# A decoder layer on one core: group scores in one piece, another order of normalisation, queries stored by head, and a lead-in with three weight buffers

## The chip, the cores and the metric

The kernel runs on one core of one Trainium2 chip. The metric is the time of one execution in device microseconds (us). Profiles are of one execution each, with all times counted from the start of its span.

## The reference, cut to what matters

Eight sequences of 128 tokens with 512 features pass three residual blocks, each followed by a layer norm: a gated block with a polynomial part and a feed-forward part, cross-attention against a context, and a last feed-forward block. The change lies in the cross-attention:

```python
x = _rmsnorm(hidden_states, ln_weight)
h_q = (x @ w_q.T).reshape(b, lq, H, DH)                  # H = 32 heads of DH = 128
h_k = (key_value_states @ w_k.T).reshape(b, lk, H, DH)
h_v = (key_value_states @ w_v.T).reshape(b, lk, H, DH)
score = jnp.einsum('bqhd,bkhd->bhqk', h_q, h_k) + position_bias[None]
score = jnp.where(m, score, -jnp.inf)
score = jax.nn.softmax(score, axis=-1)
attn = jnp.einsum('bhqk,bkhd->bqhd', score, h_v).reshape(b, lq, H * DH)
return hidden_states + attn @ w_out.T
```

The inputs' mask leaves only keys among the last 32 of each sequence, and the kernel finds that out at run time. It then takes the branch `attention(few=True)`, the one that runs here.

## The kernel before

The eight sequences are two halves of four. The attention runs 64 head steps `n`: heads 0 to 15 of half 0 (n 0 to 15), the same heads for half 1 (n 16 to 31), heads 16 to 31 of half 1 (n 32 to 47), then of half 0 (n 48 to 63). In the first and third of these blocks (`shared(n)`), keys and values of both halves are computed at once; in the second and fourth (called late here) they come from what was kept, so those steps have no `keys` and `values` products, only semaphore steps. The last six steps of a late block ahead of a shared one have the keys of the heads to come.

Every engine walks an order written out by hand, a cycle per `n`. In cycle `n` TensorE (PE) has:

- `queries(n + 5)`: the small keys of a head times `wq`, in float32, into `bank[0]`. ScalarE (ACT) copies it to `t_ring` (`copy_queries`, L1133), with the head as the innermost index, so that consecutive elements are 16 bytes apart.
- `keys(n + 6)`: `few_hi`/`few_lo` times `wk_hi`/`wk_lo`, three products for each of four chunks, into `bank[1]`. It waits for the ACT copy of the bank (`copy_keys`), and for the two rounded parts of the weights: `split_k` on ACT (L1034) and `rest_k` on VectorE (DVE), made from `wk`, two buffers loaded by SyncE (SP).
- `turn(n - 1)` (L755) transposes the normalised probabilities, `weigh(n - 2)` (L822) adds to the output in `acc`, `outer(n - 1)` (L800) multiplies values and output weights, `values(n)` makes values.
- `group_scores`: the scores of four heads together (a group), 16 float32 products of 128 columns in `bank[2]` (32 passes, L728) on top of the bias (L706). With `j = n % 4`, the first half (part 0) stands at the end of the cycle `j == 2` and the second half (part 1) in the cycle `j == 3`, behind `queries`.

DVE, in cycle `n` with `m = n + 1`, has `add_mask(m)` (L1511; only for `m % 4 == 0` at this place, the others are done ahead), `find_max(m)` (L1517, L1519), then `divide(n)` (L1526 to L1532), then `rest_k` and more masks. `divide(n)` needs `exponentials(n)` of ACT (L1148), which follows `copy_outer(n - 2)` and `copy_values(n - 1)` in ACT's queue. `residual(2)` and `residual(3)` of DVE at n = 17 and n = 49 free `acc` for the next block.

The lead-in (n = -6 to -1) begins while the last tiles of the block before end: `chunk(0, 3)` of ACT, then `split_k(0)`, then on PE `keys(0)`, the last `down`, and cycles of `queries` and `keys`. SP's queue holds, ahead of it, ten loads of weights and biases, then the load of `ctxF` (the few keys of the context) into `a_raw[0]`; `split_few` (L1027) rounds it.

## Time and profile before

| what | value |
|---|---|
| median of 3 runs | 781.97 us (780.22 to 782.78) |
| the profiled execution | 781.2 us, span 779.4 us |
| PE busy | 724.6 us, 93% of the span |
| DVE busy | 528.5 us, 68% |
| ACT busy | 436.6 us, 56% |
| mean granted PE clock | 0.989 |

A busy PE is a modelled duration that contains the pipeline's latency, so an interval between starts tells more than the busy share. "Idle before" names what ended the idle time ahead of an instruction. In the chain that ended last, each row starts where the one before it released it; "issue" is time for which the profile shows no releaser.

### The profile page before, as it was taken

The page shows a single profiled execution, that of the slowest core. Times are in us where ns is not written, and L with a number is a line of the kernel's source. Part 1 is how long each engine was busy: PE and PEld are TensorE (multiplying, and loading weights), DVE is VectorE, ACT ScalarE, POOL GpSimd, SP SyncE. Part 2 cuts the span into 40 slices and gives each one's busy share as a digit, 9 for nine tenths or more (in the row PEclk, how much of TensorE's full clock was granted, in tenths as well). Part 3 has the DMA queues.
Part 4 walks back from the last instruction along what each step waited for, and adds up shares of the span by engine and source line. Part 5 has one row for each costly group of instructions (what it writes and reads, how often), then busy time and mean ns, then how long its engine had stood idle before and what let it go on. Part 6 is the DMA issues. An engine that isn't in the chain of part 4 may idle for free.

```text
span 779.4 us, 12293 instructions
## 1 busy us (share of the span) xinstructions
PE 724.6 (93%) x4082; PEld 558.9 (72%) x4082; DVE 528.5 (68%) x912; ACT 436.6 (56%) x747; POOL 95.6 (12%) x84
## 2 busy tenths in 40 slices
PE   8999999999978999999989999999989779998994
PEld 6788888888868777765556777876545347886883
DVE  6556687577645786468776668656986737578655
ACT  6333233333346787777776777667767454554452
POOL 2000000190007300000000000000040002304503
PEclk9999999999999999999999999999999999999998
DMA  8555441466735665678886676566875512442631
GB/s 317 161 226 181 137 147 56 150 202 200 242 122 181 200 215 177 202 232 273 263 282 198 214 244 196 188 219 227 279 252 181 158 68 81 154 136 87 212 133 54
DMA packets 70681, 145.10 MB, mean 186 GB/s; under 512 B 7920, under 2 KB 8192, under 8 KB 69984
## 3 DMA queue, kind: packets, MB, share of 16 engines
q1 hardware_dynamic: 69200, 137.26, 54.0%
q0 software_dynamic: 1200, 6.70, 2.2%
q8 instruction: 34, 0.56, 0.3%
q10 hardware_dynamic: 224, 0.39, 0.2%
q14 instruction: 23, 0.19, 0.1%
HBM read 142.23 MB, written 2.10 MB: 185 GB/s over the span
## 4 chain that ended last, share of the span: by engine, by line
PE 74%; DVE 14%; issue 4%; DMA 3%; ACT 2%; SPq 1%; POOL 1%; ACTq 0%; DVEq 0%; POOLq 0%
PE bank L524 34%; PE acc L524 14%; PE bank L728 7%; PE acc L822 6%; PE bank L693 5%; PE bank L800 5%; DVE score L1511 2%; DVE score L1519 2%; DVE neg_max L1517 2%; DVE row_sum L1526 2%; DVE prob L1532 1%; PE bank L706 1%; DMA a_raw<-ctxF 1%; DVE a_lo L1260 1%; DMA b_raw<-b 1%
## 5 line engine op out<-in xcount | busy, mean ns | idle before, releaser
L524 PE MATMUL bank<-feat_hi,a_hi 128*128 128x512 f32 x348 | 137.4, 395 | 3.2 <-DVE a_lo L1260 1.2
L524 PE MATMUL bank<-feat_lo,a_hi 128*128 128x512 f32 x348 | 136.3, 392 | 2.4 <-issue 2.4
L1260 DVE TENSOR_TENSOR a_lo<-a_raw,a_hi 128x1024 fp32r<-128x1024 f32 (+3 forms) x47 | 56.8, 1208 | 99.1 <-ACT a_hi L974 88.0
L1511 DVE TENSOR_TENSOR score<-bank,mask_add 128x512 f32<-128x512 f32 x64 | 42.5, 685 | 79.6 <-PE bank L728 79.6
L524 PE MATMUL acc<-b_hi,tile_hi 128*128 128x512 f32 x224 | 87.8, 392 | 4.1 <-DVE tile_lo L1260 2.2
L1133 ACT ACTIVATE t_ring<-bank 128x512 f32<-128x512 f32 x64 | 70.4, 1101 | 32.7 <-PE bank L693 32.7
L524 PE MATMUL acc<-b_hi,tile_lo 128*128 128x512 f32 x224 | 87.2, 389 | 0.0
L524 PEld LDWEIGHTS bank<-feat_hi,a_hi 128*128 128x128 f32 x348 | 65.8, 189 | 23.8 <-issue 4.3
L822 PE MATMUL acc<-u_sb,prob_t 32*128 32x512 f32 x512 | 77.2, 646 | 0.4 <-DVE resid L1368 0.4
L524 PEld LDWEIGHTS bank<-feat_lo,a_hi 128*128 128x128 f32 x348 | 65.8, 189 | 13.5
L991 ACT ACTIVATE tile_hi<-pair 128x512 fp32r<-128x512 f32 x54 | 33.9, 628 | 67.0 <-DVE pair L1322 37.3
L524 PE MATMUL bank<-feat_hi,a_lo 128*128 128x512 f32 x180 | 70.1, 390 | 0.0
L432 POOL TENSOR_SCALAR scale<-moments 128x4 f32<-128x4 f32 (+1 forms) x9 | 2.1, 233 | 542.2 <-DVEq L1390 542.0
L728 PE MATMUL bank<-t_ring,xn 128*128 128x128 f32 x512 | 62.2, 275 | 0.0
L728 PEld LDWEIGHTS bank<-t_ring,xn 128*128 128x128 f32 x512 | 60.9, 192 | 1.3
L1167 ACT ACTIVATE u_sb<-bank 128x512 f32<-128x512 f32 x64 | 38.3, 598 | 32.3 <-PE bank L800 29.6
L524 PE MATMUL acc<-b_lo,tile_hi 128*128 128x512 f32 x136 | 52.9, 389 | 0.0
L524 PEld LDWEIGHTS acc<-b_hi,tile_hi 128*128 128x128 f32 x224 | 42.2, 188 | 14.4 <-DVE b_lo L1260 3.3
L1000 ACT ACTIVATE gated<-bank 128x512 f32<-128x512 f32 x20 | 11.9, 598 | 67.8 <-PE bank L524 67.8
L1260 DVE TENSOR_TENSOR b_lo<-b_raw,b_hi 128x512 fp32r<-128x512 f32 x56 | 40.0, 715 | 14.1 <-ACT b_hi L981 13.8
L981 ACT ACTIVATE b_hi<-b_raw 128x512 fp32r<-128x512 f32 x56 | 34.8, 624 | 26.0 <-PE acc L524 21.3
L1141 ACT ACTIVATE prob_t<-bank 128x512 f32<-128x512 f32 x64 | 40.4, 631 | 15.5 <-PE bank L755 15.5
(149 smaller groups left out, 1580.2 us busy)
## 6 DMA issues: line engine op xcount, KB each, us to landing
wk<-ax SPq DMA_DIRECT2D x64, 256.0 KB, 3.5
wqi<-ax SPq DMA_DIRECT2D x64, 256.0 KB, 3.3
wq<-wqn SPq DMA_DIRECT2D x64, 256.0 KB, 3.7
wv<-wvh SPq DMA_DIRECT2D x64, 256.0 KB, 3.6
wo<-bx SPq DMA_DIRECT2D x64, 256.0 KB, 3.6
a_raw<-w SPq DMA_DIRECT2D x22, 512.0 KB, 4.1
a_raw<-a SPq DMA_DIRECT2D x21, 512.0 KB, 5.3
b_raw<-b SPq DMA_DIRECT2D x34, 256.0 KB, 2.6
```

The lines of the kernel that those rows point to most:

```text
L524: mm = pe.matmul(out_ap, w, x, start=start and k == 0, stop=stop and k == len(products) - 1, skip_group_check=True)
L693: mm = pe.matmul(bank[0][:, c * P:(c + 1) * P], wq[par][:, c * P:(c + 1) * P], few_keys, start=True, stop=True)
L728: mm = pe.matmul(bank[2][:, b * P:(b + 1) * P], xn[half][:, c, b * SEQ:(b + 1) * SEQ], t_ring[g % 2][:, c, b, :, :].rearrange("p k h -> p ...
L800: mm = pe.matmul(bank[1][:], few_values, wo[slot][:], start=True, stop=True)
L822: mm = pe.matmul(acc[b][:], prob_t[par][rows, 0:P], u_sb[par][rows, :], start=begins, stop=ends, skip_group_check=True)
L981: act.activation(b_hi[par][:], b_raw[par][:], ACT.Copy).then_inc(b_hi_ok, 1)
L991: act.activation(tile_hi[par][:], src, ACT.Copy).then_inc(tile_hi_ok, 1)
L1133: act.activation(t_ring[n // GH % 2][:].rearrange("p c b k h -> p (c b k h)")[:, n % GH:GH * N:GH], bank[0][:], ACT.Copy).then_inc(t_ok, 1)
L1141: act.activation(prob_t[n % 2][:], bank[3][:], ACT.Copy).then_inc(turned_ok, 1)
L1167: act.activation(u_sb[n % 2][:], bank[1][:], ACT.Copy).then_inc(u_ok, 1)
L1260: return dve.tensor_tensor(out_ap, whole, high, ALU.subtract)
L1511: dve.tensor_tensor(score[n % GH][:], bank[2][:].rearrange("p (b k) -> p b k", b=HB), mask_add[j][:, half * HB:(half + 1) * HB, :], ALU.ad ...
```

## The change

Nothing is computed differently; the order, the layout and the buffers change.

1. `group_scores` is one piece at the end of the cycle `j == 2`, ahead of the `queries` of the next cycle.
2. DVE has `divide(n)` ahead of `add_mask(n + 1)` and `find_max(n + 1)` where `n + 1` begins a group.
3. `t_ring` is stored head by head, so ACT writes 512 neighbouring elements; the scores' product reads it so, and writes its 128 columns into `bank[2]` with a step of four elements (16 bytes).
4. Lead-in: `wk` gets a third buffer (`gated`, free by then), so `load_k(n)` runs three ahead; the keys of n = 1, 3, 5 go to `bank[3]`; `keys` stands ahead of `queries` and waits for the copy of two steps before; `split_k`/`rest_k` run two steps ahead; on SP, `ctxF` stands behind four loads and not behind ten.

```diff
-WO_RING = 4
+WO_RING, WK_RING = 4, 3
+def keys_in(n):
+    return 3 if n < LEAD_K and n % 2 == 1 else 1
-        t_ring = two("t_ring", [P, C, HB, FEW, GH])
+        t_ring = two("t_ring", [P, GH, C, HB, FEW])
+        wk.append(gated)
 def load_k(n):
-                if n >= 2:
-                    sp.wait_ge(k_mm, n - 1)
-                sp.dma_start(wk[n % 2][:], ax[head_of(n)][:, D:]).then_inc(wk_dma[n % 2], 16)
+                if n == WK_RING - 1:
+                    sp.wait_ge(hidden_ok, HALVES * F1)
+                if n >= WK_RING:
+                    sp.wait_ge(k_mm, n - WK_RING + 1)
+                sp.dma_start(wk[n % WK_RING][:], ax[head_of(n)][:, D:]).then_inc(wk_dma[n % WK_RING], 16)
 # SP, ahead of the loop
-            for n in range(2):
-                load_k(n)
-                load_q(n)
-                load_v(n)
-                load_o(n)
-                load_bias(n)
+            load_k(0)
+            load_q(0)
+            load_k(1)
             sp.wait_ge(a_lo_ok, A30)
             sp.dma_start(a_raw[0][:], ctxF).then_inc(few_dma, 16)
-            for n in range(2, WO_RING):
+            load_q(1)
+            for n in range(2):
+                load_v(n)
+                load_bias(n)
+            load_o(0)
+            load_k(2)
+            for n in range(1, WO_RING):
                 load_o(n)
 # SP, in the loop
-                if 2 <= n + LEAD_K + 2 < HN:
-                    load_k(n + LEAD_K + 2)
+                if WK_RING <= n + LEAD_K + WK_RING < HN:
+                    load_k(n + LEAD_K + WK_RING)
 # PE, keys(n)
                     if n == 0:
                         pe.wait_ge(hidden_ok, HALVES * F1)
+                    elif n == 1:
+                        pe.wait_ge(xn_ok, C)
                     else:
-                        pe.wait_ge(k_ok, n)
-                        pe.wait_ge(kept_k_ok, shared_count(n - 1))
+                        copied = n if n >= LEAD_K else n - 1
+                        pe.wait_ge(k_ok, copied)
+                        pe.wait_ge(kept_k_ok, shared_count(copied - 1))
 # PE, group_scores
-                    for b in range(2 * part, 2 * part + 2):
+                    for b in range(HB):
                         for c in range(C):
-                            mm = pe.matmul(bank[2][:, b * P:(b + 1) * P], xn[half][:, c, b * SEQ:(b + 1) * SEQ],
-                                           t_ring[g % 2][:, c, b, :, :].rearrange("p k h -> p (k h)"), start=False, stop=(c == C - 1),
+                            mm = pe.matmul(bank[2][:, b * P:(b + 1) * P].rearrange("p (k h) -> p h k", h=GH),
+                                           xn[half][:, c, b * SEQ:(b + 1) * SEQ], t_ring[g % 2][:, :, c, b, :], start=False, stop=(c == C - 1),
                                            skip_group_check=True)
 # PE, the order of a cycle
+                    if n < 0:
+                        keys(n + LEAD_K)
                     if 0 <= n + LEAD_T < HN:
                         queries(n + LEAD_T)
-                    if few and j == 3 and n >= -1 and g + 1 < HALVES * GROUPS:
-                        group_scores(g + 1, 1)
-                    if not late and n + LEAD_K < HN:
+                    if n >= 0 and not late and n + LEAD_K < HN:
                         keys(n + LEAD_K)
                     if few and j == 2 and g + 1 < HALVES * GROUPS and n >= -2:
-                        group_scores(g + 1, 0)
+                        group_scores(g + 1)
 # ACT
-                act.activation(t_ring[n // GH % 2][:].rearrange("p c b k h -> p (c b k h)")[:, n % GH:GH * N:GH], bank[0][:],
-                               ACT.Copy).then_inc(t_ok, 1)
+                act.activation(t_ring[n // GH % 2][:, n % GH].rearrange("p c b k -> p (c b k)"), bank[0][:], ACT.Copy).then_inc(t_ok, 1)
             split_k(0)
+            split_k(1)
             few_bias_heads()
-                if late and n + LEAD_K < HN and not shared(n + LEAD_K):
+                if n < 0 or late and n + LEAD_K < HN and not shared(n + LEAD_K):
                     copy_keys(n + LEAD_K)
+                if n < 0:
+                    split_k(n + LEAD_K + 2)
                 if 0 <= n + LEAD_T < HN:
                     copy_queries(n + LEAD_T)
-                if n + LEAD_K + 1 < HN and shared(n + LEAD_K + 1):
+                if n > 0 and n + LEAD_K + 1 < HN and shared(n + LEAD_K + 1):
                     split_k(n + LEAD_K + 1)
 # DVE
-                if 0 <= m < HN:
-                    if m % GH == 0:
-                        add_mask(m)
+                if 0 <= m < HN and m % GH > 0:
                     find_max(m)
                 if n >= 0:
                     divide(n)
-                if n + LEAD_K + 1 < HN and shared(n + LEAD_K + 1):
+                if 0 <= m < HN and m % GH == 0:
+                    add_mask(m)
+                    find_max(m)
+                if n < 0:
+                    rest_k(n + LEAD_K + 2)
+                elif n > 0 and n + LEAD_K + 1 < HN and shared(n + LEAD_K + 1):
                     rest_k(n + LEAD_K + 1)
```

## Rows read from the trace of the kernel before

**Rows 1.** The page: busy time, share of the span and instructions of each engine
```profile
PE 724.6 (93%) x4082; PEld 558.9 (72%) x4082; DVE 528.5 (68%) x912; ACT 436.6 (56%) x747; POOL 95.6 (12%) x84
```
**Rows 2.** Busy us (count) by stretch: PE, PEld, DVE, ACT, POOL; clock, DMA share, GB/s
```profile
262.00:347.50 85.50, 83.51 (x608) 65.76 (x605) 57.88 (x109) 63.41 (x122) 0.56 (x2) 1.00 0.65 207
347.50:434.40 86.90, 80.29 (x514) 54.27 (x514) 63.54 (x122) 61.29 (x108) 0.00 (x0) 1.00 0.77 252
...
541.40:630.60 89.20, 76.54 (x455) 45.45 (x453) 68.17 (x133) 57.84 (x99) 9.59 (x6) 0.98 0.62 202
```
**Rows 3.** Chain that ended last, one late group: start us, us, what
```profile
373.48 0.70 DVE score L1511
...
385.44 0.39 PE bank L755
...
388.43 1.78 PE bank L728 x16
390.22 0.89 PE bank L693 x8
...
392.93 0.70 DVE score L1511
```
**Rows 4.** Timeline of DVE in that group: start, us, line, op
```profile
375.54 0.68 DVE L1526 TENSOR_REDUCE row_sum<-prob 128x4 f32<-128x512 f32 x1
...
377.27 0.68 DVE L1511 TENSOR_TENSOR score<-bank,mask_add 128x512 f32<-128x512 f32 x1
```
**Rows 5.** Timeline of ACT: exponentials of the first head of groups 4 and 5
```profile
356.15 0.62 ACT L1148 ACTIVATE prob<-score 128x512 f32<-128x512 f32 x1
...
376.69 0.63 ACT L1148 ACTIVATE prob<-score 128x512 f32<-128x512 f32 x1
```
**Rows 6.** The chain, where group 4's scores are read
```profile
351.99 0.70 DVE score L1511
```
**Rows 7.** Pieces of the chain without a releaser, ahead of `values` and of `keys`
```profile
333.56 0.58 issue
...
419.03 1.59 issue
```
**Rows 8.** Timeline of PE, first cycle of the second shared block
```profile
444.24 0.39 PE L755 MATMUL bank<-ident_r,prob 128*128 128x128 f32 x1 [0.83 <-DVE prob L1532]
```
**Rows 9.** Group 13: DVE's timeline at its scores, then the chain five cycles on
```profile
567.39 0.69 DVE L1511 TENSOR_TENSOR score<-bank,mask_add 128x512 f32<-128x512 f32 x1 [1.35 <-PE bank L728]
...
581.24 1.87 PE acc L822 x8
```
**Rows 10.** Timelines of the lead-in: ACT, PE, then DVE at the first scores
```profile
217.81 1.06 ACT L1027 ACTIVATE a_hi<-a_raw 128x1024 fp32r<-128x1024 f32 x1 [3.43 <-DMA a_raw<-ctxF]
...
221.30 0.67 ACT L1017 ACTIVATE xn<-bank,const 128x512 f32<-128x512 f32 x1
...
223.46 0.55 PE L524 MATMUL bank<-a_hi,wk_hi 128*128 128x256 f32 x1 [3.50 <-DVE wk_lo L1260]
...
247.49 0.69 DVE L1511 TENSOR_TENSOR score<-bank,mask_add 128x512 f32<-128x512 f32 x1 [4.14 <-PE bank L728]
```
**Rows 11.** The chain in the lead-in: queries, a load, queries two cycles on
```profile
232.36 1.16 PE bank L693 x8
...
234.98 3.54 DMA wk<-ax
...
239.88 1.16 PE bank L693 x8
```
**Rows 12.** Groups by line, op and tile: busy us, mean ns, idle before
```profile
L1133 ACT ACTIVATE t_ring<-bank 128x512 f32<-128x512 f32 x64 | 70.4, 1101 | 32.7 <-PE bank L693 32.7
L728 PE MATMUL bank<-t_ring,xn 128*128 128x128 f32 x512 | 62.2, 275 | 0.0
L1126 ACT ACTIVATE k_ring<-bank 128x512 f32<-128x512 f32 x64 | 38.1, 595 | 0.0
L524 PE MATMUL bank<-a_hi,wk_lo 128*128 128x256 f32 x128 | 36.6, 286 | 0.0
```

More of the change, by code:

```diff
@@ L210, in decoder_kernel @@
         wqi_dma, wq_dma = [sem("wqi_dma0"), sem("wqi_dma1")], [sem("wq_dma0"), sem("wq_dma1")]
-        wk_dma, wv_dma = [sem("wk_dma0"), sem("wk_dma1")], [sem("wv_dma0"), sem("wv_dma1")]
+        wk_dma, wv_dma = [sem(f"wk_dma{i}") for i in range(WK_RING)], [sem("wv_dma0"), sem("wv_dma1")]
         wo_dma = [sem(f"wo_dma{i}") for i in range(WO_RING)]
@@ L646, in keys @@
                 def keys(n):
-                    half, par = half_of(n), n % 2
-                    pe.wait_ge(wk_dma[par], 16 * (n // 2 + 1))
+                    half, par, raw = half_of(n), n % 2, n % WK_RING
+                    keys_bank = bank[keys_in(n)]
+                    pe.wait_ge(wk_dma[raw], 16 * (n // WK_RING + 1))
                     if shared(n):
@@ L665, in keys @@
                         if few:
-                            mm = passes(bank[1][:, 0:HALVES * P], wk_hi[par][:, chunk], wk_lo[par][:, chunk],
+                            mm = passes(keys_bank[:, 0:HALVES * P], wk_hi[par][:, chunk], wk_lo[par][:, chunk],
                                         few_hi[:, c, :], few_lo[:, c, :], c == 0, c == C - 1)
                         else:
-                            mm = pe.matmul(bank[1][:], wk[par][:, chunk], ctx_raw[half][:, c * N:(c + 1) * N],
+                            mm = pe.matmul(keys_bank[:], wk[raw][:, chunk], ctx_raw[half][:, c * N:(c + 1) * N],
                                            start=(c == 0), stop=(c == C - 1))
@@ L743, in head_scores @@
                     for b in range(HB):
-                        mm = pe.matmul(bank[2][:, b * P:(b + 1) * P], t_ring[g % 2][:, b, :, :, j].rearrange("p b k -> p (b k)"),
+                        mm = pe.matmul(bank[2][:, b * P:(b + 1) * P], t_ring[g % 2][:, j, b, :, :].rearrange("p b k -> p (b k)"),
                                        k_ring[:, n % RING, b * SEQ:(b + 1) * SEQ], start=False, stop=True, skip_group_check=True)
@@ L765, in values @@
                     if n == 0:
-                        pe.wait_ge(xn_ok, C)
+                        pe.wait_ge(k_ok, LEAD_K)
+                        pe.wait_ge(kept_k_ok, LEAD_K)
                     else:
@@ L1029, in split_k @@
             def split_k(n):
-                act.wait_ge(wk_dma[n % 2], 16 * (n // 2 + 1))
+                act.wait_ge(wk_dma[n % WK_RING], 16 * (n // WK_RING + 1))
                 if n >= 2:
                     act.wait_ge(k_mm, n - 1)
-                act.activation(wk_hi[n % 2], wk[n % 2][:], ACT.Copy).then_inc(wk_hi_ok, 1)
+                act.activation(wk_hi[n % 2], wk[n % WK_RING][:], ACT.Copy).then_inc(wk_hi_ok, 1)
             def split_v(n):
@@ L1122, in copy_keys @@
                         act.wait_ge(t_mm, n - BLOCK + 1)
-                    act.activation(kept_k[n % BLOCK], bank[1][:, other * P:(other + 1) * P], ACT.Copy).then_inc(kept_k_ok, 1)
+                    act.activation(kept_k[n % BLOCK], bank[keys_in(n)][:, other * P:(other + 1) * P], ACT.Copy).then_inc(kept_k_ok, 1)
                 if n >= RING:
                     act.wait_ge(score_mm, n - RING + 1)
-                act.activation(k_ring[:, n % RING, :], bank[1][:], ACT.Copy).then_inc(k_ok, 1)
+                act.activation(k_ring[:, n % RING, :], bank[keys_in(n)][:], ACT.Copy).then_inc(k_ok, 1)
             def copy_queries(n):
@@ L1186, in _ @@
                     chunk(2, 2 * (n - FEATURES_2), bank[0])
-                if not late and n + LEAD_K < HN:
+                if n >= 0 and not late and n + LEAD_K < HN:
                     copy_keys(n + LEAD_K)
@@ L1501, in _ @@
             rest_k(0)
+            dve.wait_ge(tile_lo_ok, T30)
+            rest_k(1)
             few_bias_rests()
```

20 lines of the change are left out of this document (9 added, 11 removed).

## The prediction

> **What bounds the kernel now.** I first read the busy time of the page: PE 93%, DVE 68%, ACT 56% [rows 1]. That is a mean over stages, so the stretches come next [rows 2]. In the first shared block PE is busy for 83.5 of 85.5 us. In the late blocks it is busy for 80.3 of 86.9 us and 76.5 of 89.2 us, while DVE has 63.5 and 68.2 us of work: neither is full, so they wait for each other in turn. The chain shows how [rows 3]: a group's scores end, DVE reads them at 373.48, stays on the chain until 385.44 when PE can transpose, PE then runs up to the next scores, which DVE reads at 392.93. One turn of this loop is 392.93 - 373.48 = 19.45 us. It contains two things that the change takes out of it: DVE's `divide` of the last head of the old group, and PE's `queries` between the two halves of the scores. The lead-in has its own loop of loads, rounding and copies [rows 10, 11].
>
> **The late loop.** `divide` goes ahead of `add_mask`. It costs 377.27 - 375.54 = 1.73 us of DVE [rows 4], and fits into the time in which DVE waits for the scores now. What it needs, the exponentials of that head, come from ACT while PE has the scores to do. So 1.73 us leave the chain. `queries` (390.22 to 391.11, 0.89 us) stand ahead of the second half now [rows 3]; behind the scores they are in nobody's way at first: another 0.89 us, 2.62 together.
>
> Part of it is given back. The `queries` now delay the `turn`, `weigh` and `outer` behind them by 0.89 us against the end of the scores. ACT's exponentials of the new group's first head stand behind the copy of that `outer`. They begin at 376.69 and take 0.63, so they end 3.8 us after the scores are read [rows 3, 5]. With 0.89 more that is 4.7 to 4.8 us. DVE wants them after `add_mask`, `find_max`, one more `add_mask` and one more `find_max`; in today's order the `divide` of 1.73 us lies between and it asks at 379.32 - 373.48 = 5.84 us, in the new order at 4.1. It waits 0.65 us. Net 2.62 - 0.65 = 1.97 us per boundary.
>
> Not all boundaries are like that one. By groups:
>
> - Scores of groups 6, 7 and 15 as the next ones (three regular loops): 3 x 1.97 = 5.9.
> - Groups 5 and 13: the cycle behind the scores belongs to a shared head, with `values` ahead of `outer`. There the exponentials end at 356.15 + 0.62, 4.8 us after the read at 351.99 [rows 5, 6]; 0.89 more makes 5.7 against a demand at 4.1, so 1.57 us come back: 2 x 1.05 = 2.1.
> - Group 8 (the last of a late block): `keys` waits 1.59 us for rounded weights that DVE makes behind `divide` [rows 7]. Those are ready in time once the DVE loop is shorter. I take 1.6, and PE is the bound from there on.
> - First shared cycle after it: `turn` sat 0.83 us for DVE's probabilities [rows 8], 1.0 with its latency. That goes.
> - Group 14: `residual(3)` and `variances(2)` fill DVE ahead of the scores. It is idle for only 1.35 us before them [rows 9], less than the 1.73 + 0.89 it would need. Net 1.35. The same loop has a `weigh` of 1.87 us where 1.07 is usual, with the granted clock at 0.98 [rows 2, 9]. PE ran at its lower level there, after a row of waits. I count half of that cost of 1.6 us as regained: 0.8.
> - After the last scores no `queries` are left and no wait comes back: 1.7.
>
> Sum of the late loop: 5.9 + 2.1 + 1.6 + 1.0 + 1.35 + 0.8 + 1.7 = 14.5 us. PE does not cut it: the stretch 347.5 to 434.4 loses 6.6 us by this, as much as it shows PE idle, and a PE counted as busy holds latency besides.
>
> **Queries by head.** A copy of one bank to neighbouring places takes 595 ns; `t_ring` takes 1101 [rows 12]. So each of the 64 copies gains 0.5 us, all on ACT. ACT has room (61 of 87 us [rows 2]), so most of them are worth nothing. The exception is a head step with `values` and no `keys`, where `values` waits 0.58 us for the copy of `turn`, which ACT does behind `t_ring` [rows 7]. The chain has three such pieces before the first late block and four before the second: 7 x 0.5 = 3.5. One more copy lies on the chain near n = 10: 0.5. Together 4.0 us.
>
> The other side of this layout is the product itself, which now writes with a step of 16 bytes in PSUM. No row shows such a write. What rows show is the pace: 16 passes of 128 float32 columns take 1.79 us [rows 3], 112 ns each and 0.87 ns a column, while the float32r product of `keys` runs 256 columns within a duration of 286 ns against 275 for these 128 [rows 12]: float32 columns come at about half the float32r pace. The nearest row for a step of 16 bytes is ACT's, 1101 against 595, a factor of 1.85. If that factor sits on the write's own pace, it disappears under the slower float32 columns and costs nothing. If it multiplies the pass, it costs 512 x 112 ns x 0.85 = 49 us. I take nothing and keep the other as a rival. The read of `t_ring` stays in runs of 32 neighbours.
>
> The Trainium skill speaks against this edit ("PSUM — Partial Sum Buffer", section "Specifications (TRN2)"): cachelines of 8 bytes, and "any non-contiguous AP slows matmuls significantly". By it the sum would come out slower than before, as in the rival of that name; no row here shows such a write.
>
> **The lead-in.** PE is idle 3.50 us up to 223.46, waiting for `rest_k(0)`, behind ACT's copy at 221.30, behind the `split_few` that waited 3.43 us for `ctxF` [rows 10]. With six loads fewer ahead (SP issues one in about 0.45 us) it lands in time, and what is late next is PE's last transposes, just before PE fell idle at 219.96. The copy behind them starts 1.3 us sooner, `keys(0)` 1.5 sooner with its `split_k` right behind.
>
> After that, two cycles take 239.88 - 232.36 = 7.52 us now, 3.76 each, in a loop with one load of 3.54 us [rows 11]. With the third buffer a load is asked for a cycle sooner, but on SP it stands behind `load_q`, which waits for `queries`. Issues 0.85, load 3.54, two roundings 1.3, semaphores 0.1: 5.8 us for two cycles, 2.9 each. The cycle of the last `down` is PE's own in both. Three cycles gain 0.85 each, 2.5 us. The first late load (n = 4) holds ACT's queue, with `copy_queries` behind it, for about 1.7 us. Net 1.5 + 2.5 - 1.7 = 2.3 us. From nothing (the lower clock lasts as long as now, or the wait on `hidden_ok` at the head of SP's queue holds `wo` loads) to 4.0.
>
> Moving `load_k(2)` behind a wait on `hidden_ok` queues three `wo` loads and the loop behind it; their first reader is `outer(1)`, which comes after the first scores (247.49 [rows 10]), so it costs nothing. The other reordered loads are read no sooner than in the second cycle.
>
> **Sum.** 14.5 + 4.0 + 2.3 = 20.8 us, against the profiled execution of 781.2 us: 760.4. The median of three runs lies 0.8 above it: about 761 us. The bounds of the gains alone are 11 us (no lead-in gain, no regained clock, exponentials half a microsecond later at each boundary) and 30 us (full 2.62 at all nine boundaries, 4 in the lead-in): 752 to 771.
>
> **Rivals.**
> 1. *The stepped write slows the scores.* One place, 512 passes, all on the path in shared blocks where PE is full. At ACT's factor: 781.97 + 49 - 20.8 = 810 us; it decides from 20.8/512 = 41 ns a pass, 112 becoming 153. For it: no contiguous run is left in a write. Against it: half pace of float32. Chance 0.14.
> 2. *Half of the gain.* DVE's loop shortens, but another wait takes its place: the exponentials behind `outer` in ACT's queue, since each boundary has only 1.97 left of 2.62 by my count. If all ACT copies there slip by another microsecond, nine boundaries lose 9 us: 770 to 776. Chance 0.13. No change within 0.3%, which is about what a measurement can tell here: 0.03.
> 3. *More than the sum.* With fewer waits PE keeps its higher clock everywhere and the lead-in gains 4 us: 750 to 754. Chance 0.10.
> 4. *The forecast*, 754 to 769: chance 0.60.
>
> Faster 0.83, same 0.03, slower 0.14. The likeliest case spans 754 to 769; I give 751 to 771.
>
> **What the profile of the changed kernel would show.** `t_ring` copies near 0.60 us on ACT. Scores as 32 passes in about 3.57 us, mean 275 ns; if the mean is nearer 400 or the 32 passes take over 5 us, rival 1 holds. DVE's wait for the scores near 2 us with `row_sum` ahead of it, and a short wait for ACT's exponentials in its place. The late loop at 17.5 us for 19.45. The 0.58 us pieces gone. The first `keys` at about 222 us, the first `add_mask` 2 to 3 us before 247.5. The prediction is wrong if the passes slow, or if the late loop stays above 18.5 us.

## The result, and the profile after

The changed kernel takes 770.77 us (median of 4 runs, 767.9 to 770.99) against 782.38 us for the kernel before on the same chip (780.22 to 783.97): a ratio of 0.9845, 95% interval 0.9811 to 0.9879. It is faster by 11.6 us where 20.8 were forecast. The profiled execution took 770.99 us, with a span of 769.2 us and a mean granted clock of 0.983. Against the profiled execution of before that is 10.2 us of span.

The first lines of the page after, engines with busy time and share, answer to [rows 1]:

```profile
PE 724.1 (94%) x4082; PEld 561.6 (73%) x4082; DVE 534.2 (69%) x912; ACT 407.1 (53%) x747; POOL 93.4 (12%) x84
```

ACT has 30 us less to do, which is the copy of `t_ring` and little else. The windows of the same three stages as in [rows 2], placed by the new starts (columns as there):

```profile
264.00:348.00 84.00, 83.38 (x609) 65.31 (x609) 60.35 (x111) 57.52 (x122) 0.57 (x2) 1.00 0.64 207
349.00:430.10 81.10, 78.35 (x514) 53.93 (x514) 64.41 (x122) 53.91 (x108) 0.00 (x0) 1.00 0.80 273
535.00:618.50 83.50, 73.63 (x454) 44.74 (x453) 68.55 (x133) 52.30 (x99) 9.77 (x6) 1.00 0.64 215
```

PE was idle for 6.6 us of the first late block before and is for 2.8 us now, and the last stretch has the full clock where it had 0.98. So the middle of the kernel did about what was forecast in kind. Where the time went is plainest from a table by stage, worked out from the timelines: each entry is when the stage's first instruction starts, in us from the start of the span. "Scores 4" is the bias product ahead of the scores of group 4.

| start of | before | after | gained since the line above |
|---|---|---|---|
| last transposes ahead of the attention | 209.79 | 210.86 | -1.07 |
| first `keys` | 223.46 | 223.47 | +1.06 |
| first `turn` | 255.49 | 258.54 | -3.04 |
| scores 4 | 346.47 | 347.96 | +1.56 |
| scores 5 | 367.95 | 368.50 | +0.94 |
| scores 6 | 387.51 | 386.98 | +1.08 |
| scores 7 | 408.99 | 406.41 | +2.05 |
| scores 8 | 433.36 | 429.11 | +1.67 |
| scores 12 | 540.38 | 533.98 | +2.15 |
| scores 13 | 561.86 | 554.51 | +0.95 |
| scores 14 | 584.12 | 574.84 | +1.93 |
| scores 15 | 603.87 | 593.13 | +1.46 |
| first tile of the last block | 630.58 | 618.50 | +1.34 |
| end of the span | 779.4 | 769.2 | -1.88 |

Three stages do not fit the sum. The lead-in, from the first `keys` to the first `turn`, loses 3.0 us. A regular late loop (scores 5 to scores 6) gains 1.08 and not 1.97. The end gives 1.9 us back. The first two are followed up below.

What the stepped write and the new `t_ring` cost stands in the lines of the page after (operation, busy us, mean ns, idle before):

```profile
L741 PE MATMUL bank<-t_ring,xn 128*128 128x128 f32 x512 | 61.4, 279 | 0.0
L1147 ACT ACTIVATE t_ring<-bank 128x512 f32<-128x512 f32 x64 | 38.1, 596 | 42.8 <-PE bank L707 42.8
L1543 DVE TENSOR_REDUCE row_sum<-prob 128x4 f32<-128x512 f32 x64 | 43.7, 683 | 30.6 <-ACT prob L1161 29.1
L1528 DVE TENSOR_TENSOR score<-bank,mask_add 128x512 f32<-128x512 f32 x64 | 42.5, 684 | 17.6 <-PE bank L741 17.6
```

The copy fell from 1101 to 596 ns [rows 12]. The mean of the scores' passes is 279 ns where it was 275 before. Those 4 ns come from one group of scores in the lead-in that ran at a low clock (below). In the other groups the 32 passes take 3.57 us, as the two pieces of 16 in 1.78 us did before [rows 3]: the write with a step of 16 bytes costs nothing here. DVE used to wait 79.6 us for scores, as this line of the page of before says:

```profile
L1511 DVE TENSOR_TENSOR score<-bank,mask_add 128x512 f32<-128x512 f32 x64 | 42.5, 685 | 79.6 <-PE bank L728 79.6
```

Now it waits 17.6 us for them, and 29.1 us for ACT's exponentials ahead of `row_sum`. That is the change of waits that the prediction named, and in the late loop it has the size that was forecast:

```profile
377.90 0.69 DVE L1543 TENSOR_REDUCE row_sum<-prob 128x4 f32<-128x512 f32 x1 [0.58 <-ACT prob L1161]
```

DVE reads group 5's scores at 373.13 us, and these exponentials end at 377.86 us, 4.73 us later (4.7 to 4.8 forecast). DVE waits 0.58 us for them (0.65 forecast).

**The late loop after.** The chain that ended last, from one group's scores to the next (start, us, what), answers to [rows 3]:

```profile
369.52 3.57 PE bank L741 x32
373.09 0.89 PE bank L707 x8
...
375.17 1.07 PE bank L813 x2
376.24 0.02 issue
376.26 0.02 ACT u_sb L1180
...
376.75 0.60 ACT v_sb L1173
377.36 0.09 issue
377.45 0.36 PE bank L767
...
387.81 3.57 PE bank L741 x32
```

There is no DVE on it any more. ACT is on it three times a group, between `outer` (L813) and the next `turn` (L767). PE's own timeline shows what that costs:

```profile
377.45 0.36 PE L767 MATMUL bank<-ident_r,prob 128*128 128x128 f32 x1 [0.33 <-ACT v_sb L1173]
381.15 0.36 PE L767 MATMUL bank<-ident_r,prob 128*128 128x128 f32 x1 [0.33 <-ACT v_sb L1173]
```

From one `turn` to the next is 381.15 - 377.45 = 3.70 us. In the 1.21 us between the end of `outer` (376.24) and `turn`, PE has its `queries` to do, and then stands idle for 0.33 us. Meanwhile ACT copies `outer`'s product to `u_sb` and behind it, in its queue, bank 3 to `v_sb`, and `turn` waits for that second copy. In a late cycle nobody reads `v_sb`: `outer` takes `kept_v`. The program issues the copy all the same, and `turn`, which writes into the same bank, waits for its semaphore. I had not priced this queue position. I had priced the exponentials one place further back in it.

**The lead-in after.** PE's timeline, with the idle time before and its releaser in brackets:

```profile
223.47 0.36 PE L534 MATMUL bank<-a_hi,wk_hi 128*128 128x256 f32 x1 [2.44 <-DVE wk_lo L1275]
237.14 1.13 PE L707 MATMUL bank<-k_ring,wq 128*128 128x128 f32 x8 [1.59 <-ACT t_ring L1147]
...
243.76 0.50 PE L720 MATMUL bank<-a_hi,ident_r 128*128 128x512 f32 x1 [2.52 <-ACT t_ring L1147]
```

The first idle time is 2.44 us in place of 3.50 [rows 10]. But PE now waits for the copies of `t_ring`, and the chain says why these are late:

```profile
230.89 0.91 PE bank L707 x8
231.82 0.33 SPq L296
...
232.66 3.19 DMA wk<-ax
235.88 0.03 ACT wk_hi L1047
236.41 0.59 ACT t_ring L1147
237.14 1.14 PE bank L707 x8
239.15 3.42 DMA wk<-ax
242.59 0.63 ACT wk_hi L1047
243.22 0.49 ACT t_ring L1147
...
244.49 5.20 PE bank L741 x32
```

`queries` (L707) release `load_q` on SP (L296), behind which `load_k` is issued, whose 3.2 to 3.4 us of DMA hold `split_k` on ACT (L1047), behind which stands the copy of `queries`, for which PE waits. At 242.59 ACT rounds weights that no `keys` need for two steps, while the first scores wait for a copy that was ready to run. Then the scores take 5.20 us for the 32 passes that take 3.57 elsewhere. The granted clock tells why:

```profile
240.00:252.00 12.00, 9.37 (x62) 8.95 (x62) 3.48 (x6) 2.58 (x7) 11.22 (x10) 0.86 0.36 117
```

Its PEclk is 0.86, a mean over the two levels of 2.4 and 1.2 GHz; from 244 to 250 us, around the passes alone, it is 0.72. PE had been idle for 2.52 us just before the scores.

### The profile page after: what moved, and what is told of

The parts are those of the page before. It is cut to its first block, busy times and chain, and to the rows that moved or that the text cites. A ratio compares the mean times of both kernels' runs of the same rounds, so it can differ in the third digit from the quotient of the medians.

```text
span 769.2 us, 12295 instructions
## 1 busy us (share of the span) xinstructions
PE 724.1 (94%) x4082; PEld 561.6 (73%) x4082; DVE 534.2 (69%) x912; ACT 407.1 (53%) x747; POOL 93.4 (12%) x84
## 4 chain that ended last, share of the span: by engine, by line
PE 85%; DVE 5%; issue 3%; DMA 3%; ACT 3%; POOL 1%; SPq 1%; ACTq 0%; DVEq 0%; POOLq 0%
PE bank L534 37%; PE acc L534 16%; PE acc L835 8%; PE bank L741 8%; PE bank L813 7%; PE bank L707 5%; PE bank L767 1%; ACT v_sb L1173 1%; PE bank L720 1%; DMA b_raw<-b 1%; PE bank L566 1%; DMA wk<-ax 1%; DMA a_raw<-a 1%; POOL resid L509 1%; DVE b_lo L1275 0%
## 5 line engine op out<-in xcount | busy, mean ns | idle before, releaser
L534 PE MATMUL acc<-b_hi,tile_hi 128*128 128x512 f32 x224 | 89.5, 399 | 3.9 <-DVE tile_lo L1275 2.0
L835 PE MATMUL acc<-u_sb,prob_t 32*128 32x512 f32 x512 | 74.9, 640 | 0.0
L1543 DVE TENSOR_REDUCE row_sum<-prob 128x4 f32<-128x512 f32 x64 | 43.7, 683 | 30.6 <-ACT prob L1161 29.1
L1147 ACT ACTIVATE t_ring<-bank 128x512 f32<-128x512 f32 x64 | 38.1, 596 | 42.8 <-PE bank L707 42.8
L1528 DVE TENSOR_TENSOR score<-bank,mask_add 128x512 f32<-128x512 f32 x64 | 42.5, 684 | 17.6 <-PE bank L741 17.6
L1180 ACT ACTIVATE u_sb<-bank 128x512 f32<-128x512 f32 x64 | 38.2, 598 | 29.1 <-PE bank L813 26.4
L534 PEld LDWEIGHTS acc<-b_hi,tile_lo 128*128 128x128 f32 x224 | 42.9, 192 | 8.9
```

Of the source, the lines that this page charges most:

```text
L534: mm = pe.matmul(out_ap, w, x, start=start and k == 0, stop=stop and k == len(products) - 1, skip_group_check=True)
L835: mm = pe.matmul(acc[b][:], prob_t[par][rows, 0:P], u_sb[par][rows, :], start=begins, stop=ends, skip_group_check=True)
L1147: act.activation(t_ring[n // GH % 2][:, n % GH].rearrange("p c b k -> p (c b k)"), bank[0][:], ACT.Copy).then_inc(t_ok, 1)
L1180: act.activation(u_sb[n % 2][:], bank[1][:], ACT.Copy).then_inc(u_ok, 1)
L1528: dve.tensor_tensor(score[n % GH][:], bank[2][:].rearrange("p (b k) -> p b k", b=HB), mask_add[j][:, half * HB:(half + 1) * HB, :], ALU.ad ...
L1543: dve.tensor_reduce(row_sum[:], prob[n % 2][:], AX_X, ALU.add).then_inc(sum_ok, 1)
```

## The experiments: each part alone

Four kernels share one chip and one median of before (782.07 us). Each undoes or does one part. The first keeps the parts 1 to 3 and has the lead-in of before.

```diff
 # oldlead: the kernel before, with the scores in one piece, divide first, t_ring by head; WK_RING = 2, the old order of loads, keys and queries
 # divide: the kernel before, with this alone, on DVE
-                if 0 <= m < HN:
-                    if m % GH == 0:
-                        add_mask(m)
-                    find_max(m)
+                if 0 <= m < HN and m % GH > 0:
+                    find_max(m)
                 if n >= 0:
                     divide(n)
+                if 0 <= m < HN and m % GH == 0:
+                    add_mask(m)
+                    find_max(m)
 # together: the kernel before, with group_scores in one piece at the end of the cycle j == 2, and nothing else
 # layout: the kernel before, with t_ring [P, GH, C, HB, FEW], ACT's copy in 512 neighbours, and the scores' product written with the step of four
```

> Parts 1 to 3 with the lead-in of the kernel before. Theory L (the new lead-in costs time: ACT holds copy_queries behind split_k, which waits for wk, and PE falls to its lower clock): about 2 us faster than the changed kernel, near 769 us, first turn near 255 us. The ledger on record (the new lead-in gains 2.3): 2.3 us slower than the changed kernel, near 773.

> Only the divide of the old group ahead of add_mask. The ledger: 1.73 us less at each late boundary and no wait for the exponentials (3.8 against a demand at 4.1 us): 9 x 1.5 us, near 769. Theory V (in late cycles turn waits for the copy of v_sb, which stands behind the copy of u_sb in ACT's queue, so the loop PE, ACT is nearly as long as DVE's): less than half of it, 4 to 6 us, near 777.

> Only the scores of a group in one piece. The ledger: 0.89 us at each boundary where DVE's chain binds, exponentials still in time: 8 us, near 774. Theory V: the same, since the DVE chain still has the divide in it; a gain under 3 us speaks for another bound.

> Only t_ring by head and the stepped write of the scores. The ledger: 4 us (seven waits of 0.58 us shortened, one copy), near 778. Rival that the stepped write slows the scores: over 5 us a group for 32 passes, slower than 790; the changed kernel's trace already shows 3.57, so this should repeat. Also possible: the faster ACT queue helps late cycles too (v_sb sooner), then 775 or less.

| kernel | median us | ratio to before (95%) | first `turn` at | first `turn` to last block |
|---|---|---|---|---|
| before | 782.07 | | 255.49 | 375.09 |
| oldlead | 766.62 | 0.9798 (0.9766 to 0.9831) | 254.95 | 361.57 |
| divide | 769.35 | 0.9847 (0.9823 to 0.9871) | 253.44 | 363.52 |
| together | 775.66 | 0.9926 (0.9898 to 0.9955) | 256.08 | 369.37 |
| layout | 779.39 | 0.9965 (0.9944 to 0.9986) | 256.58 | 370.15 |

The expectations, each with its result:

- oldlead: the theory that the new lead-in costs time gave 769 us with the first `turn` near 255 us, the sum on record gave 773. It took 766.62 us, with the first `turn` at 254.95. The first theory holds, and the sum's +2.3 falls.
- divide: 769 by the sum, 777 if `turn` and `v_sb` already bound nearly as much. It took 769.35 us. With DVE still carrying the loop, the wait for `v_sb` is not yet the limit.
- together: 774 forecast, 775.66 measured.
- layout: 778 forecast, 779.39 measured.

Two things follow. First, the kernel without the new lead-in is 4 us faster than the one with it: 766.62 against 770.77. The scores of group 1 begin at 264.62 against 268.37 us, those of group 5 at 364.75 against 368.50: 3.75 us apart at both places, so the difference was made ahead of them. Second, between the first `turn` and the last block the parts gain 11.6, 5.7 and 4.9 us alone, 22.2 together, and 13.5 us when they are all there. Part of that difference is the clock and not the parts. Between the scores of group 13 and those of 14 the granted clock was 0.94 in before and 0.93 in oldlead, and 1.00 in divide, together, layout and the changed kernel. So that one loop counts 1.94, 1.31 and 1.32 us in the three kernels with one part and only 0.46 us in oldlead. Without it the parts gain 9.6, 4.4 and 3.6 us alone, 17.7 together, against 13.1 us in oldlead and 13.2 us in the changed kernel. The overlap is thus 4.5 us. The loop from scores 5 to scores 6 shows it: 19.56 us before, 18.92 in divide, 18.92 in together, 19.43 in layout and 18.50 in oldlead. Each part shortens the same loop, and another limit is reached when the first of them is in.

The layout alone gives 4.9 us there, and that this is close to the 4.0 of the prediction is in part luck: 3.25 us come where they were forecast (first `turn` to scores 4, and scores 8 to 12), 1.3 us from the clock between scores 13 and 14. Its passes of 128 columns are written with the step and its total is not slower. A part of divide's time over the whole is luck: its lead-in has the code of before, and its first `turn` came 2 us earlier, with a granted clock of 1.00 from 222 to 228 us where before had 0.72. The stretch behind the first `turn` leaves that out.

## The experiments: the lead-in

Two kernels take the changed kernel and move one step in one queue each.

```diff
 # copyfirst: ACT, in the loop; the copy of queries no longer waits behind the rounding that waits for a load
-                if n < 0:
-                    split_k(n + LEAD_K + 2)
                 if 0 <= n + LEAD_T < HN:
                     copy_queries(n + LEAD_T)
+                if n < 0:
+                    split_k(n + LEAD_K + 2)
 # loadfirst: SP, in the loop; load_k no longer waits behind load_q, which waits for queries
+                if n < 0:
+                    load_k(n + LEAD_K + WK_RING)
                 if 2 <= n + LEAD_T + 2 < HN:
                     load_q(n + LEAD_T + 2)
-                if WK_RING <= n + LEAD_K + WK_RING < HN:
+                if 0 <= n and n + LEAD_K + WK_RING < HN:
                     load_k(n + LEAD_K + WK_RING)
```

> The changed kernel, in the lead-in with copy_queries ahead of split_k in ACT's queue. Theory Q (PE's 5.6 us of waits for the t_ring copy come from that copy standing behind a split_k that waits for its load): the four waits go, the first scores start 2 to 3 us sooner, PE may keep its clock there; 768 to 766 against 770.8. Theory D (the loop of loads binds, the order of ACT only moves the wait to keys and wk_lo): within 1 us of the changed kernel.

> The changed kernel, in the lead-in with load_k ahead of load_q in SP's queue. Theory D: the loads of wk start as soon as keys are done and not after queries plus two issues, 1.5 to 2.5 us sooner per load, so split_k waits for none: 3 to 4 us faster than the changed kernel, near 767. Theory Q: also faster, since split_k then waits for nothing and the copy behind it goes through; the two theories differ in the run with the other order, not in this one. If the lower clock alone is the cause, within 1 us.

The kernel with the copy first took 766.79 us (ratio 0.9791, 0.9756 to 0.9825), the one with the load first 763.18 us (0.9753, 0.9730 to 0.9777; before 782.89). The first scores began at 241.41 and 240.40, against 243.76. With the load first the same place of the chain reads:

```profile
241.13 3.57 PE bank L743 x32
```

and the window of that stretch:

```profile
240.00:252.00 12.00, 10.55 (x87) 10.30 (x88) 6.97 (x12) 6.14 (x12) 11.55 (x10) 1.00 0.53 170
```

The 32 passes take 3.57 us again and the granted clock is 1.00. In copyfirst the window from 240 to 252 us has 1.00 too. With the copy first, theory Q came true (scores 2.4 us sooner, 766 to 768 us), and theory D's "within 1 us" fell: a copy behind a rounding that waits for a load is what held PE. With the load first the gain was larger than either theory's 767 us. Its first `turn` came 5.6 us sooner than in the changed kernel, and some 2.8 us of the profile came in the last block, for a reason that has nothing to do with the lead-in (see the end of the span, below). Both moves mend the same wait, and either does most of it.

The third buffer was worth about what the prediction gave it, once the load is not queued behind another: the first `turn` stands at 252.99 us against 254.95 with the old lead-in, 2.0 us. The medians differ by more, 763.18 and 766.62 us, but were taken on two chips, and oldlead's profile holds the low clock between scores 13 and 14.

## The experiments: the late loop

My next idea was that the late loop is held by `outer` and its copy, ahead of `values`, and that the order of the shared cycles (`values` first, then `outer`) would free it. This was run on the kernel with the old lead-in (values_first), and on the changed one with both moves of the lead-in (all_three).

```diff
 # values_first (and all_three): PE
-                    if late:
-                        outer(n - 1)
                     if 0 <= n < HN:
                         values(n)
-                    if n >= 1 and not late:
+                    if n >= 1:
                         outer(n - 1)
 # ACT
-                if late:
-                    copy_outer(n - 1)
                 if n >= 0:
                     copy_values(n)
-                if n >= 1 and not late:
+                if n >= 1:
                     copy_outer(n - 1)
```

> Parts 1 to 3 with the old lead-in, and in late cycles values ahead of outer on PE and copy_values ahead of copy_outer on ACT. Theory V (turn waits for the v_sb copy behind the u_sb copy): a late loop of 18.5 us becomes 16.8 to 17.5, some 6 to 9 us over the eight late loops: 758 to 761 against 766.6. The ledger (exponentials and DVE bind, V is no bound): within 1 us of 766.6, since the exponentials stay behind the copy of outer.

> The changed kernel with all three orders: copy_queries first, load_k first, values first. If the new lead-in's loss is the two queue orders and its third buffer is worth anything, it ends below values_first by 1 to 3 us. If the third buffer is worth nothing, it equals values_first.

Both fell short. The first took 775.30 us (0.9912, 0.9879 to 0.9945; before 782.89), 8.7 us more than oldlead, and the second 773.61 us (0.9881, 0.9856 to 0.9907), 1.7 us below values_first as expected, but slower than the changed kernel in spite of the mended lead-in. A regular loop became 19.72 us in values_first, where it is 18.48 with the order of the changed kernel. Its chain:

```profile
375.64 0.51 issue
376.15 1.10 PE bank L798 x2
...
378.28 0.36 PE bank L753
```

`outer` (L798) starts 0.51 us after `weigh` each time, and the chain shows no releaser. In the code `values(n)` now stands ahead of it, which in a late cycle is only semaphore steps, one of them a wait for the copy of `turn` to `prob_t`. ACT's timeline has that copy behind those of `k_ring` and `t_ring`, ending at 375.80 us:

```profile
375.19 0.61 ACT L1134 ACTIVATE prob_t<-bank 128x512 f32<-128x512 f32 x1
375.88 0.60 ACT L1153 ACTIVATE v_sb<-bank 128x512 f32<-128x512 f32 x1
```

`outer` follows at 376.15 us. From one `turn` to the next this makes 378.28 - 374.22 = 4.06 us out of 3.70: in the old place `outer` was the work that covered this copy. So PE's old order was not what held the loop, and the new one lengthens it.

This loop is not the whole loss. Of the 10.9 us between oldlead and values_first from the first `turn` to the last block, 6.1 us lie behind the last scores, where PE's granted clock was low:

```profile
612.00:626.30 14.30, 10.25 (x33) 4.61 (x29) 6.23 (x13) 5.57 (x11) 0.00 (x0) 0.52 0.25 92
```

In those last cycles the edit also moves `outer` behind the `features` products, and its copy behind `chunk`. Whether that or something else lowered the clock there is not shown.

What was left of the theory was ACT's own order. Two kernels test that alone: v_early, on top of both_orders (both moves of the lead-in), and narrow_v, on top of loadfirst.

```diff
 # both_orders: the changed kernel with copyfirst and loadfirst
 # v_early: both_orders, and on ACT
-                if late:
-                    copy_outer(n - 1)
                 if n >= 0:
                     copy_values(n)
+                if late:
+                    copy_outer(n - 1)
 # narrow_v: loadfirst, and in copy_values on ACT
-                act.activation(v_sb[n % 2][:], bank[3][:], ACT.Copy).then_inc(v_ok, 1)
+                width = N if shared(n) else 1
+                act.activation(v_sb[n % 2][:, 0:width], bank[3][:, 0:width], ACT.Copy).then_inc(v_ok, 1)
```

> The changed kernel with load_k first and copy_queries first. Theory D and Q together: all_three had its first turn 1 us sooner than loadfirst; 1 us less than loadfirst, near 762. If the orders overlap fully, 763.

> loadfirst with the v_sb copy of late cycles cut to one column (this leaves out a copy whose values nothing reads in this branch). Theory V (in late cycles turn waits for the v_sb copy behind the u_sb copy): the regular late loop of 18.5 us falls to the 17.5 of the ledger, where exponentials and DVE bind; some 6 us less in all, near 757 against 763.2. If the loop stays at 18.5, the wait put down to v_sb is another one.

> The changed kernel with load_k first, copy_queries first, and only on ACT the late copy_values ahead of copy_outer (PE keeps its order; its semaphore step for values is issued while outer still runs). Theory V: the v_sb copy runs under outer, turn finds it done, the late loop falls to 17.5; with 1 us from the lead-in, 755 to 757. Against it: v_sb's copy waits for PE's step and for the turned copy and delays the u_sb copy, as in values_first; then 18.5 or more and over 762.

| kernel | median us | ratio to before (95%) | regular late loop us | first `turn` to last block us |
|---|---|---|---|---|
| both_orders | 764.37 | 0.9776 (0.9760 to 0.9793) | 18.49 | 359.97 |
| narrow_v | 761.08 | 0.9743 (0.9720 to 0.9766) | 17.88 | 356.70 |
| v_early | 760.44 | 0.9727 (0.9710 to 0.9745) | 17.73 | 356.36 |

The moved copy gives 3.6 us behind the first `turn`, most of it in the two late blocks, and the copy cut to one column 3.1 us against loadfirst (359.84). The bank and the semaphore are the same in all of them, so the cost is the time at which this copy ends: its place behind another and its length. The mechanism holds; its size was put too high. Six us and a loop of 17.5 us were expected, and 755 to 757 us in all. The loops in front of scores 5 and 8 gained nothing by the move (20.53 and 22.69 us).

v_early against all_three tests PE's order: ACT has `copy_values` ahead of `copy_outer` in both, and only all_three has `values` ahead of `outer` on PE (with `copy_outer` behind `chunk` in the last cycles). They take 760.44 and 773.61 us. Both moves of the lead-in together are no better than the load first alone (764.37 against 763.18, where 762 to 763 were expected), which agrees with their mending one wait. The chain of v_early over a loop:

```profile
363.12 3.57 PE bank L743 x32
...
369.83 0.89 PE bank L709 x8
370.72 0.14 issue
370.86 0.36 PE bank L769
...
380.85 3.57 PE bank L743 x32
```

From these scores to the next takes 17.73 us, and PE is on the chain throughout but for some 0.3 us. ACT's copy to `v_sb` now comes first:

```profile
372.52 0.60 ACT L1175 ACTIVATE v_sb<-bank 128x512 f32<-128x512 f32 x1
373.38 0.60 ACT L1182 ACTIVATE u_sb<-bank 128x512 f32<-128x512 f32 x1 [0.27 <-PE bank L815]
```

This is the fastest kernel of the study: 760.44 us, 10.3 us below the changed one, with three places in a queue moved. In a regular late loop little is left but PE's own products, so with this work on PE it is close to the floor.

## The experiment: the stepped write

The scores' passes are float32, and the argument that a slow write would disappear under them says nothing about faster products. So the kernel with the load first was given stepped writes at two more places: `outer`'s product of 512 float32 columns with a step of 16 bytes, and the float32r product of `keys` in runs of two elements 32 bytes apart. The columns land in another order at both places, so this kernel does not compute the reference's output and serves for its times alone.

```diff
-mm = pe.matmul(bank[1][:], few_values, wo[slot][:], start=True, stop=True)
+mm = pe.matmul(bank[1][:].rearrange("p (k h) -> p h k", h=GH), few_values, wo[slot][:], start=True, stop=True)
-mm = passes(keys_bank[:, 0:HALVES * P], wk_hi[par][:, chunk], wk_lo[par][:, chunk],
+mm = passes(keys_bank[:, 0:HALVES * P].rearrange("p (k h d) -> p h k d", h=4, d=2), wk_hi[par][:, chunk], wk_lo[par][:, chunk],
```

> loadfirst with two more products that write with a step: outer (float32, 512 columns) with the scores' step of 16 bytes, and keys (float32r, 256 columns) in runs of two elements, 32 bytes apart; the columns land in another order, so the output is not the reference's. Theory H (float32 columns are so slow that a stepped write hides): outer's two passes stay at 0.86 us, and keys, at the full pace, may slow. If the stepped write costs by itself, outer's passes grow too, by up to the factor 1.85. If runs of two are free at full pace, keys stays at 1.43 us for 12 passes.

One execution: 763.9 us, with a span of 762.1 (loadfirst 760.7). The lines of the stepped kernel:

```profile
L815 PE MATMUL bank<-wo,v_sb 128*128 128x512 f32 x64 | 32.8, 594 | 0.0
L536 PE MATMUL bank<-a_hi,wk_lo 128*128 128x256 f32 x128 | 36.1, 282 | 0.0
```

and the same of the kernel with contiguous writes:

```profile
L815 PE MATMUL bank<-wo,v_sb 128*128 128x512 f32 x64 | 32.8, 594 | 0.0
L536 PE MATMUL bank<-a_hi,wk_lo 128*128 128x256 f32 x128 | 36.3, 284 | 0.0
```

594 and 594 ns, 282 and 284 ns. Since the ends of products are modelled, the intervals are the better witness, and they agree: in the chains of both kernels `outer`'s two passes take 0.86 us in the shared blocks, the products of `keys` start 0.12 us apart, and from the scores of group 1 to those of group 15 it is 324.76 us stepped and 324.77 us contiguous. Neither product notices. The 1.4 us between the spans is not from the products: the first `turn` comes 1.4 us sooner in the stepped kernel, and its last block is 2.8 us longer.

So a step of 16 bytes slowed neither of the float32 products here. Whether the slow pace of float32 hides it, as the prediction argued, is not shown: the float32r form, at twice that pace, did not slow either, but each of its runs fills eight bytes. A float32r write of single elements with a step was not tried.

## Why the prediction was right or wrong

**Direction and range: right.** 770.77 us lies within 751 to 771, 0.2 us from its upper edge. The gain is 11.6 us of 20.8. That it ended on this side of the edge is luck: two things that no part of the change sets, the clock between scores 13 and 14 and the idle stretch in the last block, move the time by 1.5 us and by up to 3 us. The time is that of its second rival (770 to 776), and so is the reason in kind: the loop shortens, and another wait takes its place in ACT's queue. That rival named the exponentials. They came as late as the sum had them and no later, and what came was the copy to `v_sb`.

**Which part holds, by its own steps.**

- *A boundary as 2.62 minus 0.65, 1.97 us net.* The step that failed in the late loop: it counted what stands in ACT's queue in front of the exponentials, and not in front of `turn`. Once DVE is off the chain, `turn` waits for `v_sb` behind `u_sb`, three times a group. Measured 1.08 us for group 6, 2.05 for 7 and 1.46 for 15, in sum 4.6 for 5.9; only group 7 gave what was forecast, and its loop is no regular one (it has the `keys` of the heads to come, 21.48 us before). The forecast loop of 17.5 us was 18.48 us from scores to scores, and 18.28 by DVE's reads (373.13 to 391.41), as the prediction took its 19.45. The prediction's own sign of being wrong, a loop that stays above 18.5 us, was all but reached. With the copy moved (v_early) the loop is 17.73. The upper bound's "nine boundaries" has one too many: there are seven scores with a late loop before them and the piece after the last.
- *Groups 5, 13, 8 and the one after.* Forecast 1.05, 1.05, 1.6 and 1.0 us. Groups 5, 13 and 8 gained 0.94, 0.95 and 1.67; the first shared cycle was seen to gain 0.5 us (scores 8 to 9: 27.69 us before, 27.17 after).
- *Group 14: 1.35 + 0.8.* Measured 1.93. The `weigh` of 1.87 us is gone and the granted clock of the stretch is 1.00. In oldlead, with the same order of work there, the lower level stayed (0.93 between these scores, 0.94 before) and the loop gained 0.46. So the lower clock, of which I had counted half as regained, went wholly in one kernel and stayed in the other. That this item came near its 2.15 is luck.
- *After the last scores: 1.7.* Measured 1.34.
- *Queries by head: 4.0.* Alone it gave 4.9 us behind the first `turn`, of which 3.25 where it was forecast. In the changed kernel the gain from the first `turn` to scores 4 was 1.56 for 2.0, and that from scores 8 to 12 was 2.15 for 3.0 with the cycle above. The 595 ns and the free write were right, though the reason given for the free write is not shown, and rival 1 is excluded: no pass slowed.
- *Lead-in: +2.3.* The second wrong step. The first piece was 1.1 us and not 1.5, and the first `keys` stood at 223.47 and not at 222. The step saw that `load_k` stands behind `load_q`, let the loop run at 2.9 us a cycle all the same, and charged 1.7 us to ACT's queue for one late load. There were two late loads, of 3.19 and 3.42 us, and each held a copy of `queries` that PE asked for. PE idled, and its clock fell for the scores. The first `add_mask`, forecast 2 to 3 us ahead of 247.5, came at 249.73. The stage lost 3.0 us. With the load ahead of `load_q` the same buffers gave 2.0 us against the old lead-in and 2.5 us against before, what the sum had.
- *The end of the span: nothing.* It gave back 1.9 us. PE meets an idle stretch at the start of the last block in all kernels, and its length differs. In the chain of before:

```profile
641.15 2.40 issue
```

and of after:

```profile
629.09 3.60 issue
632.69 7.82 PE bank L534 x22
...
646.09 3.63 PE bank L534 x16
```

The idle stretch is 1.2 us longer. After it twelve products in a row start about 0.43 us apart, seven in before, where the later ones start 0.23 us apart, which is another 1.0 us. Across all fourteen kernels here the stretch was 2.15 to 3.62 us with no relation to the parts they have (layout 2.15, together and loadfirst 2.30, before 2.40, divide 2.71, both_orders 2.78, oldlead 3.17, copyfirst 3.61, stepped 3.62).

The instructions show no releaser for it, but the DMA packets of the traces point at one. In each of the fourteen traces the queue that loads instructions (q8 in the page) has a packet of 16 KB that starts between 0.4 us before the stretch and 1.4 us after its begin, and PE goes on 1.2 to 1.5 us after that packet has ended. In layout it starts 0.07 us before and takes 1.06 us, and PE is idle for 2.15 us; in the changed kernel it starts 1.38 us after and takes 0.92 us, and PE is idle for 3.60 us. So the stretch looks like a wait for code, and its length is set by when that packet is sent. This is read from timing alone: 34 such packets pass in an execution, most of them beside a busy PE, and no run here changed the code's place or size to test it.

The sum as it should have been, in gains between before and after: lead-in -3.0 and not +2.3; the late loops and layout 15.1 and not 18.5; the end -1.9 and not 0. The start up to the first `keys` is even: the trace after ran 1.1 us late ahead of it, and then won the 1.1 us of the first wait. That is 10.2 us of span.

**What the parts share.** The three parts behind the first `turn`, alone, gave 22.2 us and together 13.5; without the loop in which only the clock differed, 17.7 and 13.1. The prediction's sum had two of them in one loop (2.62 less what comes back), but not the limit they meet there: the wait for `v_sb` at 18.5 us, and below it a loop that PE fills, at 17.7. A part's gain alone is no term of a sum.

## What to carry to other kernels

When a change takes an engine off the chain, walk the queue of the next engine in it for every waiting step, and not only for the one that it was made for: here one of the five copies of ACT's cycle, read by nobody, held the late loop at 18.5 us instead of 17.7, and moving it past one other was worth 4 us. When a load is started earlier, look at what stands ahead of it in the queue that issues it, and at what stands behind its first reader: a rounding done two steps ahead holds the copy that is wanted now. Parts that act on one loop are to be measured together, since what each gains alone does not add. Compare stage by stage before you credit a part with a total: here the clock in one loop and an idle stretch in the last block moved totals by 1.5 us and by up to 3 us, whatever the parts.

## What the runs showed of the hardware

**A stepped write into PSUM is free here.** 128 float32 columns with a step of 16 bytes, 512 with the same step, and 256 float32r columns in runs of two 32 bytes apart took what their contiguous forms take (32 passes in 3.57 us; 594 and 594 ns; 282 and 284 ns). The Trainium skill ("PSUM — Partial Sum Buffer", section "Specifications (TRN2)") says that any non-contiguous pattern slows matmuls significantly, on account of cachelines of 8 bytes. The measurements do not agree, for these three forms; the third writes eight bytes in a run, so it says nothing of single float32r elements. ACT's write to SBUF with that step does cost: 1101 against 596 ns for 512 elements.

**A short idle stretch can cost more than its length.** After an idle time of 2.52 us the 32 passes of the scores took 5.20 us for 3.57, with a granted clock of 0.86 in 12 us around them; without that idle time the same stretch was at 1.00. That is 1.6 us on top of 2.5. It was not the only idle time there: PE had waited 1.59 and 0.42 us shortly before. At the start of the last block the same was seen after 3.60 us of idle time: 22 products in 7.82 us, 355 ns each, where 16 of them take 3.63 us, 227 ns each, later on. The granted clock was 0.76 from 628 to 642 us. Not every such stretch costs this, and its length alone does not tell: after 2.40 us of idle time in before the granted clock was 0.88 (640 to 654 us), after 2.30 us in loadfirst it was 1.00 (622 to 636 us).
